# The gates' product with the experts' output biases, from f32 with 8 rows to bf16 with 48 rows

## What is computed

```
gates = jax.nn.softmax(x @ Wg + bg, axis=-1)
hmid = jax.nn.relu(jnp.einsum('bsh,ehd->bsed', x, W1) + b1)
eout = jnp.einsum('bsed,edh->bseh', hmid, W2) + b2
y = jnp.einsum('bse,bseh->bsh', gates, eout)
return x + y
```

## Time and profile before

| | busy us | share of span | instructions |
|---|---|---|---|
| TensorE, products | 930.4 | 91% | 7937 |
| TensorE, weight loads | 764.3 | 74% | 7937 |
| VectorE | 622.8 | 61% | 1966 |
| ScalarE | 573.0 | 56% | 966 |
| GpSimd | 281.7 | 27% | 357 |

### The profile page before, as it was taken

How to read it: one execution, slowest core, us unless ns; L and a number is a source line. 1 busy time by engine, 2 the same in 40 slices (tenths; PEclk the granted TensorE clock), 3 DMA queues, 4 the chain that set the end, 5 groups by cost and what they waited for, 6 DMA issues and landing times.

```text
span 1026.9 us, 20378 instructions
## 1 busy us (share of the span) xinstructions
PE 930.4 (91%) x7937; PEld 764.3 (74%) x7937; DVE 622.8 (61%) x1966; ACT 573.0 (56%) x966; POOL 281.7 (27%) x357
## 2 busy tenths in 40 slices
PE   3677998988999999999999999999999996999960
PEld 2444555555679888989988989889988985889960
DVE  7778786778468657265554546546455665862226
ACT  2287778775886556364464455545455562754420
POOL 6946144310200111021123222022321103147660
PEclk9689999999999999999999999999999998999995
DMA  6334443352970000000000000000000013023318
GB/s 160 122 126 139 149 138 122 111 197 65 231 181 17 1 1 2 1 1 6 16 2 21 1 17 6 2 22 1 22 1 11 12 42 103 19 57 94 86 37 248
DMA packets 85386, 66.47 MB, mean 65 GB/s; under 512 B 8113, under 2 KB 75814, under 8 KB 85290
## 3 DMA queue, kind: packets, MB, share of 16 engines
q1 hardware_dynamic: 80868, 56.87, 19.2%
q0 software_dynamic: 4352, 8.28, 2.5%
q10 hardware_dynamic: 70, 0.02, 0.0%
HBM read 33.82 MB, written 31.59 MB: 64 GB/s over the span
## 4 chain that ended last, share of the span: by engine, by line
PE 75%; ACT 10%; DVE 9%; issue 3%; DMA 1%; POOL 1%; SPq 0%; POOLq 0%; ACTq 0%; DVEq 0%
PE psum L1396 24%; PE psum L1373 18%; PE psum L1228 4%; PE psum L1166 3%; DVE maxes L1739 2%; PE psum L1136 2%; PE psum L1209 2%; ACT big L2293 1%; PE psum L1287 1%; PE psum L1329 1%; PE psum L1307 1%; PE psum L1242 1%; PE psum L1182 1%; PE psum L1448 1%; PE psum L1158 1%
## 5 line engine op out<-in xcount | busy, mean ns | idle before, releaser
L1396 PEld LDWEIGHTS psum<-ew,big 128*128 128x128 f32 x2560 | 315.4, 191 | 20.6 <-ACT big L2293 4.8
L1396 PE MATMUL psum<-ew,big 128*128 128x128 f32 x2560 | 321.9, 276 | 3.4 <-ACT big L2293 2.2
L2293 ACT ACTIVATE big<-psum,cols 128x512 f32<-128x512 f32 x256 | 174.4, 687 | 165.6 <-PE psum L1373 165.0
L1373 PE MATMUL psum<-parts,q_stack 128*128 128x512 f32 x640 | 217.7, 421 | 0.6 <-ACT big L2300 0.5
L1739 DVE TENSOR_REDUCE maxes<-psum 128x4 f32<-128x1024 f32 (+1 forms) x96 | 113.5, 1218 | 20.5 <-PE psum L1182 20.1
L1859 DVE SCALAR_TENSOR_TENSOR hT<-psum,gates,hT 128x128 f32<-128x128 f32 x256 | 71.8, 344 | 89.2 <-PE psum L1396 88.9
L1373 PE MATMUL psum<-parts,k_stack 128*128 128x512 f32 x320 | 125.8, 393 | 0.0
L2560 POOL DMA_INDIRECT routed<-big,slot_i x64 | 62.7, 979 | 228.1 <-DVE slot_i L2048 183.5
L1373 PEld LDWEIGHTS psum<-parts,q_stack 128*128 128x128 f32 x640 | 106.3, 190 | 12.9 <-ACT big L2300 0.7
L2570 POOL DMA_INDIRECT answers<-hT,to x64 | 62.2, 972 | 60.9 <-DVE hT L2067 41.6
L1373 PEld LDWEIGHTS psum<-parts,k_stack 128*128 128x128 f32 x320 | 60.0, 188 | 13.6
(11 more groups left out here) (381 smaller groups left out, 1586.9 us busy)
## 6 DMA issues: line engine op xcount, KB each, us to landing
q_stack<-q_pieces SPq DMA_DIRECT2D x32, 192.0 KB
k_stack<-k_pieces SPq DMA_DIRECT2D x32, 192.0 KB
routed<-empty_row SPq DMA_DIRECT2D x4, 1040.0 KB, 11.9
big<-routed SPq DMA_DIRECT2D x16, 260.0 KB, 2.9
answers<-gb_tok SPq DMA_DIRECT2D x4, 1024.0 KB, 10.5
q_pieces<-gb_tok SPq DMA_DIRECT2D x16, 192.0 KB, 2.1
k_pieces<-gb_tok SPq DMA_DIRECT2D x16, 192.0 KB, 2.1
x<-in_L_attn_x SPq DMA_DIRECT2D x4, 512.0 KB, 5.9
```

The source lines that it names most:

```text
L1373: last = eng.matmul(bank(i), w1_part(wp, e)[:, fs], parts[2 * xk + xp][:, :], start=n == 0, stop=n == 2)
L1396: last = eng.matmul(psum[:, i, k * C:(k + 1) * C], hid[:, r, f, k * P:(k + 1) * P], ew2[:, e, f, :], start=f == 0, stop=f == FC - 1)
L2293: eng.activation(hid[:, held("hid", "up", n, e, f), f, :], bank(held("bank", "up", n, e, f)), ACT.Relu, bias=col("L0_ffn_b1", e * FC + f)) ...
```

## The change

The product of gates and b2 is done in bf16 pieces. A f32 number is split in three bf16 pieces, each the rounding of what the ones before leave. Of the nine products of pieces the six larger ones are kept: `PAIRS` lists them as (gate piece, bias piece), and each pair has 8 rows of its own, so the product has 48 rows.

- New step `ss_p` on GpSimd, once per unit: five operations split the gates and write each piece as often as it is used.
- `ss_t` turns these 48 columns by a bf16 product with a bf16 identity; `gT` is bf16 with 48 rows.
- `ss_b` multiplies `gT` by `b2_rows`, bf16 with 48 rows.
- New step `ss_c` on VectorE, once: it writes the bf16 identity, builds three masks of rows, and splits the biases into `b2_rows`.
- New step `b2` on the sync queue, once: six copies of b2 below one another. The load in `late` is gone.
- Estimates: `ss_t` 0.4 to 0.3 and `ss_b` 1.08 to 0.35 on TensorE.

```
-        one("ss_t", n, "pe:.4 act:.57", [("mg_n", n)] + ..., rank, chain)
-        one("ss_b", n, "pe:1.08 act:.5", [("ss_t", n)], rank, chain)
+        p.step("ss_p", n, work="pool:2", after=[("mg_n", n)] + ..., rank=rank, chain=chain)
+        one("ss_t", n, "pe:.3 act:.57", [("ss_p", n), ("ss_c",)] + ..., rank, chain)
+        one("ss_b", n, "pe:.35 act:.5", [("ss_t", n)], rank, chain)
+    p.step("b2", work="sp:3 dma:3", after=[("mrow", B - 1)])
+    p.step("ss_c", work="dve:2.4", after=[("b2",), gated])
...
+            def b2_in_rows():
+                for r in range(len(PAIRS)):
+                    eng.dma_start(b2[NE * r:NE * (r + 1), :], a["L0_ffn_b2"]).then_inc(b2_in, 16)
...
             def ss_t(n):
                 i = held("bank", "ss_t", n)
+                w.wait_ge(*done("ss_p", n))
+                w.wait_ge(*done("ss_c"))
...
-                    last = eng.transpose(psum[0:NE, i, k * P:(k + 1) * P], gates[:, t, :], ident[:, :])
+                    last = eng.matmul(psum[0:PROWS, i, k * P:(k + 1) * P], gate_pieces[:, n % 2, k, :], ident_b[:, :],
+                                      start=True, stop=True)
...
-                    last = eng.matmul(psum[:, i, k * C:(k + 1) * C], gT[:, n % 2, k * P:(k + 1) * P], b2[:, :],
+                    last = eng.matmul(psum[:, i, k * C:(k + 1) * C], gT[:, n % 2, k * P:(k + 1) * P], b2_rows[:, :],
                                       start=True, stop=True)
...
+            def ss_c():
+                w.wait_ge(consts, IDENT)
+                eng.tensor_copy(ident_b[:, :], ident[:, :])
...
+                w.wait_ge(b2_in, 16 * len(PAIRS))
+                rest = b2
+                for b in range(3):
+                    eng.tensor_copy(b2_piece[:, :], rest).then_inc(chain.sem, chain.more())
+                    w.wait_ge(chain.sem, chain.n)
+                    if b == 0:
+                        eng.tensor_scalar(b2_rows[:, :], b2_piece[:, :], picks_b2[:, 0:1], None, ALU.mult)...
+                    else:
+                        eng.scalar_tensor_tensor(b2_rows[:, :], b2_piece[:, :], picks_b2[:, b:b + 1], b2_rows[:, :], ALU.mult, ALU.add)...
+                    if b < 2:
+                        eng.tensor_tensor(b2_rest, rest, b2_piece[:, :], ALU.subtract).then_inc(chain.sem, chain.more())
...
+            def ss_p(n):
+                r, g = gate_rest[:, n % 2, :, :], gates[:, CT * n:CT * (n + 1), :]
+                w.wait_ge(*done("mg_n", n))
...
+                for piece in range(3):
+                    times = 3 - piece
+                    mine = gate_pieces[:, n % 2, :, at:at + NE]
+                    last = eng.tensor_copy(gate_pieces[:, n % 2, :, at:at + times * NE].rearrange("p t (r e) -> p t r e", e=NE),
+                                           g.unsqueeze(2).to_broadcast([P, CT, times, NE]))
+                    if piece < 2:
...
+                        eng.tensor_tensor(r, g, mine, ALU.subtract).then_inc(chain.sem, chain.more())
```

More of the change, by code:

```diff
@@ L36 @@
 EPS = 1e-5
+PAIRS = [(g, b) for g in range(3) for b in range(3 - g)]
+PROWS = len(PAIRS) * NE
 MASKED = -1e30
@@ L1107, in cols_ @@
                     w.wait_ge(*c)
-                eng.transpose(psum[:, held("bank", "cols"), 0:n], col_rows[:, :],
+                eng.transpose(psum[:, held("bank", "cols"), 0:n], col_rows[0:n, :],
                               ident[0:n, 0:n]).then_inc(sem("cols", "pe"))
```

59 lines of the change are left out of this document (43 added, 16 removed).

## The result

The changed kernel takes 1035.95 us (median of 22 runs, 1030.82 to 1039.55), the kernel before 1031.53 us beside it (22 runs, 1026.45 to 1035.97): a ratio of 1.0044, 95% interval 1.0031 to 1.0057. That is 4.5 us slower, inside the half per cent that was called no change, and distinguishable from none only because there are so many runs. The profiled execution took 1036.0 us (span 1034.3), that of before 1028.6 (1026.9). The latter was 2.9 us under its kernel's median, the former at its own, so the two traces lie 7.4 us apart where the medians lie 4.4.

The account below looks back on a forecast made before the run. TensorE, busy all the time from 300 us, was taken to bound the kernel. Terms +4.6 - 7.1 + 1.5 + 1.6 = +0.6 us gave 1031.0 us; own range 1026 to 1034, 8 in 10 range 1023.5 to 1036.5.

Parts of the forecast that it names:

- no change: Whole kernel: time within about 0.5%, 5.2 us, of the kernel before; chance 0.58.
- First place: Unit 0, after about 293 us: late bias rows stall TensorE and lower its clock; +4.6 us (2.5 to 7.5).
- Units 1 to 7: Gate turns and bias products on always-busy TensorE: cheaper in bf16 by 1.0 us per unit; -7.1 us (4.5 to 8.4).
- the steady stretch shortens by 6 to 8 us: Sign for the stretch where TensorE never rests: the prediction is wrong if it does not shorten by 6 to 8 us.
- Second place: Last batch's normalised tiles: the new order turns and splits the first expert's rows later; +1.5 us (0 to 2.6).
- Tail: Kernel's end: last send ends 8.5 us behind TensorE's last product instead of 6.9; +1.6 us (0 to 2).
- The bias product's busy time: Sign on TensorE: bias product under 2.5 us busy over all units instead of 9.2.
- GpSimd's split: Rival at each unit's turn: five operations exceed the 2.9 us available; at 4.5 us each, about 1042; chance 0.07.
- The late rows: Rival at unit 0: late bias rows cost nothing, giving 1022 to 1025.4 us; chance 0.24.
- bf16 is cheaper: Rival claimed the opposite for turns and bias products: 0.11 us an instruction, saving 4.5, so 1033.6; chance inside the 0.58.
- The order costs more than I read: Rival: both end terms at upper bound, full clock loss, rows at 297; +6.1 us, about 1036.5; chance 0.11.

Follow-up runs that it names:

- after: The changed kernel itself, as first measured and profiled: 1035.95 us, ratio 1.0044 to the kernel before.
- a_free: Changed kernel with the six b2 copies issued before mrow 13 and the fills reading empty_row instead of gb_tok, their wait dropped: 1029.2 us, ratio 0.9968.
- b_newlists: Kernel before, its operations unaltered, in the step order that the changed kernel's planner makes: ratio 1.0058 to the kernel before.
- b_free: Kernel before with only the fill edit: fills read empty_row instead of gb_tok, no wait for them before the copy into gb_tok: ratio 0.9995.
- a_best: a_free with the planner's TensorE estimate for ss_t at .4 instead of .3: ratios 0.9958 and 0.9947 to the kernel before.
- a_early2: Changed kernel with the six b2 copies issued before mrow 13 on the sync queue: 1034.3 us, ratio 1.0007 to the kernel before.
- kind II: Measurements where the kernel before itself took 1060.7 and 1064.9 us instead of 1031 to 1035; need not be a property of the chip.
- a_early: Changed kernel with the six b2 copies moved directly ahead of the eight fills on the sync queue: ratio 1.0048 to the kernel before.
- a_order: Changed kernel with the planner's TensorE estimate for ss_t at .4 instead of .3: ratio 1.0033 to the kernel before.
- after_again: The unaltered changed kernel measured again beside variants on the same chip: 1037.4 us, ratio 1.0041 to the kernel before.
- a_warm: Changed kernel with 40 dummy identity products on TensorE before its wait for the first unit's gate pieces: ratio 1.0048 to the kernel before.
- a_warm2: a_best with 50 dummy identity products on TensorE in the wait before batch 14's turn: ratio 0.9956 to the kernel before.
- a_warm3: a_best with 28 dummy identity products on TensorE in the wait before batch 14's turn: ratio 0.9953 to the kernel before.

## Why the prediction was right, and where it was not

The time, 1031.0, lay 5 us low; "no change" held, and 1035.95 lies in the range of 8 in 10, half a microsecond from its upper end, but outside the forecast's own 1026 to 1034. The forecast was +0.6 us, the medians say +4.4. Between the two traces, counted from the first logits, the late biases cost 8.2 us (A of after less A of a_free), unit 0's cheaper products and the order in A come to -0.3 together, what lies behind A and is not the products comes to 2.5 (0.6 - 3.2 + 4.7 + 1.2 - 0.8; the order, but for about 1 us of the 4.7, see below), and the products of units 1 to 7 bring 4.8: 5.6 in sum. The mechanisms were right. Of the four sizes two were far too small, one fitted by luck, and one was near.

- **First place, +4.6: mis-sized, 7.9 in the profile and 11.4 in the second.** The chain of causes was right to the instruction. The stop was to be 4.2 us and was 5.5. I had the first cast at 295.0; it came at 297.74, of which 1.7 is the execution's own offset and 1.0 the landing: the fills ended as far behind the first logits as before (18.2 us), and the biases 1.45 us behind the fills where I had 0.45. I took 0.8 for the clock and 2.7 were lost, the larger part of the miss; my upper bound of 1.6 was too low as well. And I took one execution's fill as fixed, while the biases' arrival moves by 3 us between two executions of one program. The upper bound of the whole, 7.5, was too low for both. The Trainium skill, "DMA: Bandwidth & Descriptors", section "Anatomy of one DMA — SWDGE (gpsimd) path", gives a transfer issued by GpSimd a fixed cost of about 2 us whatever its size; here, on the sync queue and with the fills draining until 296.3, 3.6 us passed from the last issue (294.2) to the first use.
- **Units 1 to 7, -7.1: the sum was met, by the wrong terms.** The trace pair shows -7.4 in B and C together, and I could have taken that as proof. b_newlists splits it: the products are worth -4.8, and -2.6 is the new order of steps (+0.6 in B, -3.2 in C), which I had not counted at all. The steps that failed are the 0.06 us per bf16 instruction (0.08 measured) and the neglect of the neighbours, which lose 1.2 us. That two errors of 2.3 and 2.6 us met is luck, and it hid that the sign "the steady stretch shortens by 6 to 8 us" does not test the arithmetic.
- **Second place, +1.5: mis-sized, 4.7.** The same 863 TensorE instructions take 130.4 us instead of 125.8. TensorE idles 4.4 us instead of 1.7 behind batch 14's turn, most of it in three waits of 1.6, 0.7 and 1.4 us for results of ScalarE. The late splits standing in front of those is my reading; no run takes them apart. The lower clock, which the 6.8 us wait in front brings in both kernels, ends 5.0 us behind batch 14's turn instead of 3.0, which is about 1 us more by the half speed. That part isn't the order's: the end of the low level moves from execution to execution of one list (4.1 us behind the turn in b_free, 3.9 in a_free, 4.8 and 5.9 in the two of a_best). With it nearly equal, b_free and a_free have 126.3 and 129.8, so the order costs 3.5 there. I had looked at the one split and asked nothing about the steps that it pushes behind it.
- **Tail, +1.6: 1.2.** Right in mechanism and nearly in size: the last send ends 8.2 us behind the last product, as forecast; a_best, with the old order, has the old 6.0 us from the last product to the last send's start again.
- **Signs.** The bias product's busy time over all units is 3.2 us, not under 2.5, the same error as the 0.06. GpSimd's split takes 3.05 us for unit 0, over the 2.9 that I had set as a limit, and it costs nothing there, since the pieces lay ready 13.7 us before the turn.
- **Rivals.** The late rows cost all that they showed: a_early2 and a_free give it back at the end. GpSimd's split never held TensorE up. bf16 is cheaper, 0.08 us where I had bounded it by 0.04 and 0.11. "The order costs more than I read" was the closest of them, and its 1036.5 the closest time: it was for a stop of this size and both ends dear, though it had only 0.11.

What stays open: why kind II is slower in C and E, where TensorE idles 28.7 us in E of a_early and 11.2 in a_early2, the same list. The mean granted clock of its runs is lower too (0.95 against 0.96), which can be cause or effect of the idling. a_order's B, 1.5 us longer than in any other of the changed kernels, has the granted clock of 0.95 beside it, and nothing tells why the clock was so in that execution.

## What to carry to other kernels

A wait may have a second one right under it: look in the trace for every wait, even one of 0.2 us, at the place that you are about to delay, since moving the first source only uncovers it. A planner that sees cheaper steps moves everything behind them, and its moves were here, stage by stage, as large as what the arithmetic saved; run the old operations in the new order before crediting either. Count a mixed group by starts, with the groups on both sides of it, not by its own durations. A stage that shortens by the forecast amount proves nothing while two causes act in it.

## What was not expected of the hardware

- Eight bf16 instructions of 48 rows or columns took 0.65 us start to start between f32 ones. The f32 groups beside the bf16 turn took 0.17 us more per unit than beside an f32 turn; beside the product of few rows they were as long with f32 (8 rows) as with bf16 (48).
- An idle stop of 5.5 us was followed by 5.6 us of work at the 1.2 GHz level (after), one of 8.7 us by 6.2 (after_again). With TensorE kept at work through the stop the level stayed at 2.4 GHz throughout (a_warm, a_warm2). The length of one stop does not settle it: behind 2.4 us of idle in a_early2 the level stayed at 2.4 GHz, behind 2.2 us in a_warm3 it stood at 1.2 GHz for 3.4 us, and in b_newlists 3.4 us at 1.2 GHz came 2.1 us behind a stop of 0.9.
- In one execution (a_order) the granted clock was 0.95 for hundreds of microseconds of steady work, and B and C took 1.9 and 2.3 us more than in a_warm3, which has the same order there and is of the same kind.
- An f32 product of 128x128 by 128x128 shows as two instructions and took 0.22 us; a transpose of the same shape is one, 0.11.
- The same program took 1031 us in one set of runs and 1061 in another, 3% more. By the traces of a_early and a_early2, with one list on TensorE, all of it lies behind unit 0's last `mix`, at 442 us: 9.5 us in C and 21.2 in E.
